# The sum and the centering of the probes' norms, moved from VectorE to GpSimd

## The reference, cut to what matters

```
r = Vf @ Wg.T + bg                                   # 8 logits
pv = einsum('epd,nd->nep', Wp, Vf)                   # 8 experts x 8 probes
c = sqrt(sum(pv * pv, axis=-1)) / sqrt(8)            # 8 norms
s = ln(r, g_r, b_r) + sigmoid(alpha) * ln(c, g_c, b_c)
topv, sel = top_k(s, 2);  w = softmax(topv)
delta = sum over e of  w_e * (silu(Vf @ W1[e].T + b1[e]) @ W2[e].T + b2[e])
out = Vf + delta
```

## Time and profile before

| what | us |
|---|---|
| median of 3 runs | 1230.02 (1230.0 to 1231.1) |
| the profiled execution | 1230.65 |
| its span in the profile | 1228.9 |
| PE busy | 1208.4 (98%) |
| DVE busy | 996.9 (81%) |
| ACT busy | 542.5 (44%) |
| POOL busy | 547.7 (45%) |

### The profile page before, as it was taken

One profiled execution on the slowest core, in us unless ns is written; L12 is line 12 of the kernel. 1 busy time (PEld: TensorE's weight loads), 2 busy tenths in 40 slices (PEclk: granted clock), 3 DMA queues, 4 the chain that ended last, 5 costly groups with the idle time before them and its releaser, 6 DMA issues.

```text
span 1228.9 us, 18429 instructions
## 1 busy us (share of the span) xinstructions
PE 1208.4 (98%) x5712; PEld 994.0 (81%) x5712; DVE 996.9 (81%) x2276; ACT 542.5 (44%) x1127; POOL 547.7 (45%) x400
## 2 busy tenths in 40 slices
PE   8999999999999999999889999999999999999998
PEld 5888878788877787887678888888888888888887
DVE  6987788988888888876778888888888888888864
ACT  4454454544545444454434343434434344343441
POOL 1443433333333443434355464645646455464531
PEclk9999999999999999999989999999999999999999
DMA  6565444453433443443222323213132231322201
GB/s 223 163 199 183 146 146 129 138 153 104 129 112 114 127 135 105 138 125 101 74 76 63 103 68 88 95 61 104 60 95 87 69 103 61 95 85 70 87 24 45
DMA packets 128513, 131.64 MB, mean 107 GB/s; under 512 B 12232, under 2 KB 82288, under 8 KB 128416
## 3 DMA queue, kind: packets, MB, share of 16 engines
q1 hardware_dynamic: 128416, 130.47, 34.1%
HBM read 80.62 MB, written 49.81 MB: 106 GB/s over the span
## 4 chain that ended last, share of the span: by engine, by line
PE 87%; DVE 5%; ACT 3%; DMA 2%; issue 2%; SPq 0%; POOL 0%; DVEq 0%; ACTq 0%; POOLq 0%
PE ps L1551 27%; PE ps L1552 27%; PE ps L1556 27%; PE ps L1762 3%; PE ps L1754 1%; DMA q_in<-q_scratch 1%; DMA wm_in<-in_L_wmod_dram 1%; PE ps L1657 1%; DVE zk L1266 1%; ACT exp_k L837 1%; DVE qf L1242 1%; ACT exp_q L808 1%; ACT exp_q L810 1%; ACT exp_k L839 0%; DVE zk L1278 0%
## 5 line engine op out<-in xcount | busy, mean ns | idle before, releaser
L711 POOL TENSOR_TENSOR cn<-c,half 128x16 f32<-128x16 f32 x32 | 104.1, 3254 | 259.7 <-DVE c L1365 259.7
L687 POOL TENSOR_TENSOR xn_lo<-xn,xn_hi 128x512 fp32r<-128x512 f32 x64 | 86.0, 1344 | 278.9 <-ACT xn_hi L799 278.9
L808 ACT ACTIVATE exp_q<-qf 128x512 f32<-128x512 f32 x64 | 40.5, 632 | 150.7 <-DVE qf L1242 150.7
L1551 PE MATMUL ps<-g_hi,qT_hi 128*128 128x512 f32 x256 | 103.2, 403 | 1.2 <-ACT qT_hi L863 1.1
L1551 PE MATMUL ps<-wk_hi,xT_hi 128*128 128x512 f32 x256 | 101.8, 398 | 2.3 <-ACT xT_hi L793 2.3
L1551 PE MATMUL ps<-v_hi,xT_hi 128*128 128x512 f32 x256 | 103.9, 406 | 0.0
L1551 PE MATMUL ps<-k_hi,xn_hi 128*128 128x512 f32 x256 | 102.7, 401 | 0.0
L1551 PE MATMUL ps<-wq_hi,xT_hi 128*128 128x512 f32 x256 | 102.5, 400 | 0.1
L1552 PE MATMUL ps<-wq_lo,xT_hi 128*128 128x512 f32 x256 | 101.4, 396 | 0.0
L1552 PE MATMUL ps<-wk_lo,xT_hi 128*128 128x512 f32 x256 | 101.3, 396 | 0.0
L1552 PE MATMUL ps<-v_lo,xT_hi 128*128 128x512 f32 x256 | 101.1, 395 | 0.0
(11 more groups left out here) (249 smaller groups left out, 3282.4 us busy)
## 6 DMA issues: line engine op xcount, KB each, us to landing
xin<-_attn_hidden_states_dram SPq DMA_DIRECT2D x64, 256.0 KB, 3.1
q_scratch<-qf SPq DMA_DIRECT2D x64, 256.0 KB, 3.2
xin<-_attn_hidden_states_dram SPq DMA_DIRECT2D x32, 512.0 KB, 4.2
q_in<-q_scratch SPq DMA_DIRECT2D x128, 128.0 KB, 2.9
out_dram<-qf SPq DMA_DIRECT2D x64, 256.0 KB, 2.0
xn_scratch<-xn SPq DMA_DIRECT2D x62, 256.0 KB, 2.0
xq<-xn_scratch SPq DMA_DIRECT2D x248, 64.0 KB, 2.5
wm_in<-in_L_wmod_dram SPq DMA_DIRECT2D x4, 1024.0 KB, 6.0
```

What stands on the lines that cost most here:

```text
L687: nc.gpsimd.tensor_tensor(moved(xn_lo[:, 1 - s, :], i + 1), kept(xn[:, 1 - s, :], i + 1), moved(f32(xn_hi[:, 1 - s, :]), i + 1), ALU.subtr ...
L711: nc.gpsimd.tensor_tensor(cn[:].rearrange("p h e -> p (h e)"), c2[:].rearrange("p h e -> p (h e)"), half[:], ALU.pow).then_inc(cn_done, 1)
L808: nc.scalar.activation(exp_q[:, s, :], zq[:, s, :], ACT.Relu, scale=-1.0).then_inc(rq_done, 1)
L1551: nc.tensor.matmul(dst, ah, bh, start=start and n == 0, stop=False)
```

## The change

DVE's two instructions of `variances` go. POOL does their work inside `probe_norms`, right behind the power and ahead of `q_times_ks`: three additions that fold 8 values to 4, 2 and 1, a multiplication by 1/8 with a constant tile `eighth`, and a subtraction that writes the centred norms into `zf`. Each waits for the one before it. The first addition waits for the power, the last instruction also for DVE's readers of the old values. `cc_done`, for which DVE's `rsq` waits, is now given by POOL.

```diff
+        c_four = sb("c_four", [P, 2, 4], F32, late)
+        c_two = sb("c_two", [P, 2, 2], F32, late)
+        c_mean = sb("c_mean", [P, 2, 1], F32, late)
+        eighth = sb("eighth", [P, 2, 1], F32, late)
...
                 nc.gpsimd.tensor_tensor(cn[:].rearrange("p h e -> p (h e)"), c2[:].rearrange("p h e -> p (h e)"),
                                         half[:], ALU.pow).then_inc(cn_done, 1)
+                pool.wait_ge(cn_done, j + 1)
+                nc.gpsimd.tensor_tensor(c_four[:], cn[:, :, 0:4], cn[:, :, 4:8], ALU.add).then_inc(c_folded, 1)
+                pool.wait_ge(c_folded, 4 * j + 1)
+                nc.gpsimd.tensor_tensor(c_two[:], c_four[:, :, 0:2], c_four[:, :, 2:4], ALU.add).then_inc(c_folded, 1)
+                pool.wait_ge(c_folded, 4 * j + 2)
+                nc.gpsimd.tensor_tensor(c_mean[:], c_two[:, :, 0:1], c_two[:, :, 1:2], ALU.add).then_inc(c_folded, 1)
+                pool.wait_ge(c_folded, 4 * j + 3)
+                nc.gpsimd.tensor_tensor(c_mean[:], c_mean[:], eighth[:], ALU.mult).then_inc(c_folded, 1)
+                pool.wait_ge(c_folded, 4 * j + 4)
+                wait_count(pool, rsq_done, j)
+                wait_count(pool, rcg_done, j)
+                nc.gpsimd.tensor_tensor(zf[:, :, C:C + E], cn[:], c_mean[:].to_broadcast([P, 2, E]),
+                                        ALU.subtract).then_inc(cc_done, 1)
...
             q_times_ks(0)
+            nc.gpsimd.memset(eighth[:], 1.0 / E).then_inc(eighth_set, 1)
+            pool.wait_ge(eighth_set, 1)
             nc.gpsimd.memset(sx[:], SENTINEL).then_inc(b_cleared, 1)
...
             def variances(j):
 
-                dve.wait_ge(cn_done, j + 1)
-                nc.vector.tensor_reduce(csum[:], cn[:], AX.X, ALU.add).then_inc(csum_done, 1)
-                dve.wait_ge(csum_done, j + 1)
-                nc.vector.scalar_tensor_tensor(out=zf[:, :, C:C + E], in0=over(csum[:], [P, 2, E]), scalar=-1.0 / E,
-                                               in1=cn[:], op0=ALU.mult, op1=ALU.add).then_inc(cc_done, 1)
                 dve.wait_ge(cc_done, j + 1)
                 rc = zf[:, :, HID + PV:C + E]
                 nc.vector.tensor_tensor(rsq[:].rearrange("p h k e -> p h (k e)"), rc, rc, ALU.mult).then_inc(rsq_done, 1)
```

More of the change, by code:

```diff
@@ L243, in build @@
         cn = sb("cn", [P, 2, E], F32, late)
-        csum = sb("csum", [P, 2], F32, late)
+        c_four = sb("c_four", [P, 2, 4], F32, late)
+        c_two = sb("c_two", [P, 2, 2], F32, late)
+        c_mean = sb("c_mean", [P, 2, 1], F32, late)
+        eighth = sb("eighth", [P, 2, 1], F32, late)
         row_sum = sb("row_sum", [P, 2], F32, late)
@@ L369, in build @@
         hz_done = sem("hz_done")
-        csum_done = sem("csum_done")
+        c_folded = sem("c_folded")
         cc_done = sem("cc_done")
+        eighth_set = sem("eighth_set")
         rsq_done = sem("rsq_done")
```

## The result

| | median us | lowest to highest | runs |
|---|---|---|---|
| before | 1230.51 | 1229.55 to 1231.59 | 20 |
| after | 1232.53 | 1231.86 to 1233.25 | 20 |

What follows compares the result with a forecast made beforehand. PE was taken to bound nearly the whole second pass. To the median 1230.02 us it added 1.4 for the first step and 2.0 for the steady rounds (2.6 less 0.6): 1233.4 us, with 8 in 10 for 1230.9 to 1239.5.

Steps and rivals of the forecast that it cites:

- What bounds the kernel: Nearly the whole second pass: PE is busy 560.00 of 560 us and waits only 1.0 us for DVE.
- Rival 3: PE's waits for DVE: the 1.40 us per pair freed on DVE reach PE, making it faster; chance 0.04.
- The cost on POOL, F: Five dependent POOL instructions between the powers and `qks` take 1.43 us per pair.
- Rival 2: Small POOL instructions cost 1.70 us per pair, total 1241.8 us; chance 0.12 with what lies between.
- The first step, +1.4 us: First step of the second pass: `qks` starts later by the five instructions, and `xn` and PE with it, +1.4 us.
- give-back from the clock: First step: up to 0.7 us returns if PE's clock rises at the same instant as before; none was taken.
- The heir of the stall: DVE, each steady pair: `rsq`, now next, inherits the stall behind POOL's `xb`, its mean near 1.7 us instead of 0.19.
- The steady round: DVE - POOL - DVE round becomes longer than PE's pair by 0.09 us over 29 rounds: 2.6, less 0.6, is 2.0 us.
- the reserve: PE's turns of `xn` in the steady pairs: 0.61 us is left before lateness reaches PE.
- rival 1: Round stays under PE's time, only the first step paid, 1231.4 us; chance 0.39 with rounds over by less than 0.06.
- the slack of 0.95: DVE's two idle times in a steady pair, 0.52 + 0.08 and 0.27 + 0.08, soak up 0.95 us of lateness.
- PE waiting 0.1 us per pair at its turn: Sign in the profile after: PE waits some 0.1 us per pair at turn L1762 from the middle of the pass.

Runs made afterwards that it cites:

- the other pairs: Changed kernel with pair 0's sum and centering back on DVE, pairs 1 to 31 on POOL: 1231.22 us, 1.0008 against the kernel before.
- only pair 0 on POOL: Changed kernel with only pair 0's sum and centering on POOL, pairs 1 to 31 on DVE: 1233.09 us, 1.0022 against the kernel before.
- `xb` behind `rrs`: Changed kernel with POOL's `biased_x` put behind `router_scale` instead of ahead of it: 1247.61 us, 1.0139 against the kernel before.
- new tiles last: Changed kernel with its new tiles declared last and 8 unused bytes in place of `csum`, so older tiles stay put: 1231.83 us, 1.0010 against before.
- the kernel with one more instruction: Changed kernel with one more small dependent POOL instruction per pair (`c_mean` times 1.0): 1238.34 us, 1.0067 against the kernel before.

## Why the prediction was right, and where it was not

**What bounds the kernel: right.** The change gave nothing back on PE, and cost only where POOL holds up PE. Rival 3 did not come: 64 instructions less on DVE are worth nothing while the waits of PE for DVE are 1.0 us before and after.

**The cost on POOL, F: right to 0.04.** Forecast 1.43 us, measured 1.39. The shapes nobody had seen (three dimensions, a broadcast) take 0.20 and 0.21 us, spaced by 0.28, as `shift` led to expect. Rival 2, the dear case, falls.

**The first step, +1.4 us: right.** The wait went from 7.0 to 8.4. Pair 0 alone carries all of it and the other pairs none. I had taken no give-back from the clock. In these two executions PE resumes 621.38 - 619.65 = 1.73 us later (0.33 of it from ahead of the change) and makes its second turn at 626.57 instead of 625.28, 1.29 later, so 0.4 came back. But one pair of profiles can't tell that. Counted from POOL's first power of the pass, the second turn starts 12.0 to 13.2 us later in the seven profiles whose first step is that of the kernel before, 12.5 in the mean, and 13.5 to 14.3 us later, 13.8 in the mean, in the four whose `xn` is 1.4 us late (after, only pair 0 on POOL, `xb` behind `rrs`, new tiles last). The means differ by 1.3 us, so next to nothing comes back, and the instant at which the clock rises moves the step by up to 1.2 us between executions. The timed runs agree, but roughly: 1.5 us with the tiles last, where only the first step is left, in an interval of 0.1 to 2.3.

**The heir of the stall: right.** `rsq` has a median of 1.59 us (forecast 1.7) and ends 0.05 us behind `xb`; the row of `k_lo` in the first pass was the right witness. Less its own 0.19 it really began at 971.25, 0.14 us before `xb`'s row ends at 971.39 (I had taken 0.15). The rule of the Trainium skill (SBUF — State Buffer, Who interferes with whom), that the later of the two is blocked until the first has finished, holds here up to those 0.14 us.

**The steady round: this step failed.** It was "The next `c2`, and with it POOL's powers, is late by 1.04 - 0.95 = 0.09 us", and from it 29 x 0.09 less 0.6 = 2.0 us. The spacing of PE's pairs rose by 0.020 us and not by 0.09 after the reserve, and the 0.07 us of room that the round has instead are shown by the row of powers that catches up and by the kernel with one more instruction. Where the 0.16 between +0.09 and -0.07 come from, as far as the rows tell:

- F is 1.39, 0.04 less.
- In the kernel before, `rstd` waited for ACT's `veps` and not for POOL: from the start of `qks` to that of `rstd` it is 965.12 - 962.68 = 2.44 us, after it is 968.03 - 965.67 = 2.36. (`veps` ends at 965.04, 0.08 ahead of `rstd`, about the lag of any instruction that waits for a result.) These 0.08 us of hidden slack ahead of `xb` are used up by the change and were not in my sum, because the row of `rstd` shows no idle time at its end.
- 0.09 - 0.04 - 0.08 = -0.03. Of the remaining 0.04, 0.02 are PE's own pair, which I had held at 19.273 and which is 19.293 now; the last 0.02 are within the rounding and overlaps of the rows. So the scores start 0.92 us later behind the power and not 1.04 (973.36 - 961.03 = 12.33 for 970.84 - 959.43 = 11.41), while the slack of 0.95 was sized rightly: from the scores to the next power it is 19.27 - 11.41 = 7.86 us before and 19.22 - 12.33 = 6.89 in a round by itself, 0.97 less.

So rival 1 describes the steady state: the round stays under PE's time, though by another way than it names, since `rsq` is held. What the rival leaves out is the 0.6 us that came instead of my 2.0, and they are not from the instructions but from where the tiles lie. The sum that the runs show is 1.4 + 29 x 0.020 = 2.0 us.

The forecast lay 0.9 us above the measured median, and slower came out, but for 0.6 of its 2.0 us from a cause that no step of it had. There is luck in that 0.9: the forecast stood on the median of three runs, 1230.02, and the kernel before came out at 1230.51; as a cost it was 3.4 for 2.0, 1.4 too much, and the steady part, 2.0 for 0.6, was wrong in its cause too. Of what I said would show it, PE waiting 0.1 us per pair at its turn is not there.

## What to carry to other kernels

Instructions moved to an engine off the bottleneck are paid for in the steps in which that engine is on the way: look at the first step after a change of phase, and put them behind what the bottleneck waits for (this alone brought 2.0 down to 0.5 us here, and the same look at the old order brought 1.4 us). Where a round and the bottleneck are within a tenth of a microsecond of each other, a sum over rows cannot tell which is longer; one more small instruction per round, as a probe, can, and the spacing of one instruction per round shows what busy times and waits do not. Before a difference of a few hundredths per round is put down to the change itself, add an unused tile of the same size to the kernel before.

## What the hardware showed that I had not expected

- The place of tiles in SBUF changes the pace of PE by a little: 56 bytes that nothing uses, ahead of the others, make a pair 19.299 instead of 19.273 us (0.13%).
- A stall behind GpSimd looks like the cost of an instruction, but goes to the next one of its kind: `rsq` 0.18 or 1.59 or 2.41 us, `s` 0.19 or 1.82, the long ones each ending within 0.05 us of the end of `xb`.
- A power on GpSimd does not hold DVE for its whole length. Near the end of the kernel before, this power starts on POOL:

```profile
1189.66 2.90 POOL L711 TENSOR_TENSOR cn<-c,half 128x16 f32<-128x16 f32 x1 [7.02 <-DVE c L1365]
```

and while it runs, DVE makes an instruction with two inputs in SBUF in its normal time:

```profile
1189.81 0.69 DVE L1380 SCALAR_TENSOR_TENSOR hz<-th,zf 128x512 f32<-128x512 f32 x1 [0.23 <-ACT th L884]
```

The Trainium skill (SBUF — State Buffer, Who interferes with whom) says that a DVE instruction with two SBUF inputs contends with a GpSimd instruction that reads SBUF. The power reads SBUF too, so this pair of rows limits the rule: 0.15 us behind the start of a power on 16 elements DVE is no longer held, where `xb` on 1024 elements holds it nearly to its end. That it is the reading of the data that holds, and not the work on them, would fit, but is not shown. All 14 profiles have this row of `hz`, with 0.69 us, beside each of the last two powers.

- In the other order it is the power that is held. In a steady pair of the kernel before `hz` starts first, 0.16 us ahead of the power:

```profile
959.27 0.68 DVE L1380 SCALAR_TENSOR_TENSOR hz<-th,zf 128x512 f32<-128x512 f32 x1
```

There the same power takes 3.28 us and not 2.90. `hz` ends 0.52 us into it, and 0.52 less the 0.14 of above is the 0.38 that it takes longer. `rrs` likewise takes 1.39 us where `qT_lo` has just begun, and 1.01 in the kernel with `xb` behind `rrs`, where it stands first.
